# Near keys of a strided attention in tiles of 64 queries by 60 keys instead of 128 by 108

## The reference

```python
def _strided_allowed(S):
    i = jnp.arange(S)[:, None]
    j = jnp.arange(S)[None, :]
    return (j % STRIDE == 0) | (jnp.abs(i - j) <= LOCAL)
scores = jnp.einsum('bhqd,bhkd->bhqk', q, k) / jnp.sqrt(jnp.asarray(D, x.dtype))
scores = jnp.where(allowed, scores, -jnp.inf)
attn = jax.nn.softmax(scores, axis=-1)
out = jnp.einsum('bhqk,bhkd->bhqd', attn, v)
```

## Time and profile before

| | |
|---|---|
| median of 3 runs | 1085.3 us |
| the profiled execution, its own time | 1086.01 us |
| its span, first to last instruction | 1084.2 us |
| TensorE (matmuls) busy | 1028.3 us, 95% |
| VectorE busy | 933.8 us, 86% |
| ScalarE busy | 839.8 us, 77% |
| GpSimd busy | 251.2 us, 23% |
| chain that ended last | PE 76%, DVE 12%, issue 7%, DMA 2%, ACT 2% |

### The profile page before, as it was taken

The page is one execution under the profiler, slowest core; times in us unless marked ns, Lnnn a source line. Parts: engine busy times, 40 slices in busy tenths (PEclk is TensorE's granted clock), DMA queues, the critical chain, the costliest instruction groups (busy, mean ns, idle before and its releaser), DMA issues.

```text
span 1084.2 us, 27687 instructions
## 1 busy us (share of the span) xinstructions
PE 1028.3 (95%) x10694; PEld 462.7 (43%) x10695; DVE 933.8 (86%) x1162; ACT 839.8 (77%) x1590; POOL 251.2 (23%) x387
## 2 busy tenths in 40 slices
PE   4999999699999999999999999999999999999898
PEld 2666666233333333333333333333333333333487
DVE  6989897889999999999999999999999999999133
ACT  4667674288888888888888888888888888888600
POOL 2444453012212121221212122212121222212100
PEclk9999999599999999999999999999999999999999
DMA  6787878213223333333333333323343332231166
GB/s 197 227 254 252 262 250 274 54 46 88 85 83 90 98 85 93 102 91 99 97 96 109 98 99 95 104 84 108 91 113 88 105 91 82 86 85 58 48 236 239
DMA packets 166777, 134.07 MB, mean 124 GB/s; under 512 B 70492, under 2 KB 145884, under 8 KB 166636
## 3 DMA queue, kind: packets, MB, share of 16 engines
q1 hardware_dynamic: 163912, 128.06, 39.3%
q10 hardware_dynamic: 2736, 4.26, 1.2%
HBM read 71.13 MB, written 59.84 MB: 121 GB/s over the span
## 4 chain that ended last, share of the span: by engine, by line
PE 76%; DVE 12%; issue 7%; DMA 2%; ACT 2%; DVEq 0%; ACTq 0%
PE ps_attend L1228 17%; PE ps_attend L1145 12%; DVE peak_far L1087 10%; PE ps_attend L1186 10%; PE ps_project L621 7%; PE ps_attend L1235 6%; PE ps_attend L1308 5%; PE ps_attend L1156 4%; PE ps_project L679 4%; PE ps_attend L1197 3%; PE ps_project L594 3%; PE ps_attend L1163 3%; PE ps_attend L1204 2%; DMA sums<-out_rows 2%; PE ps_project L656 1%
## 5 line engine op out<-in xcount | busy, mean ns | idle before, releaser
L1087 DVE TENSOR_REDUCE peak_far<-ps_attend 128x2 f32<-128x1024 f32 x512 | 608.5, 1220 | 41.0 <-PE ps_attend L1186 30.8
L1028 ACT ACTIVATE probs<-ps_attend 128x512 f32<-128x512 f32 x1024 | 541.1, 597 | 49.5 <-PE ps_attend L1145 46.3
L1228 PE MATMUL ps_attend<-probs,v_op 128*17 128x512 f32 x2048 | 270.1, 600 | 0.5 <-issue 0.5
L1145 PE MATMUL ps_attend<-q_op,k_op 51*128 51x512 f16 x1024 | 252.1, 387 | 4.9 <-ACT probs L1028 3.3
L1186 PE MATMUL ps_attend<-k_op,q_op 48*128 48x512 f16 x1024 | 189.6, 388 | 26.1 <-DVE peak_far L1087 15.5
L1033 ACT ACTIVATE probs<-ps_attend 108x512 f32<-108x512 f32 x256 | 138.7, 594 | 34.6 <-PE ps_attend L1163 34.6
L1145 PEld LDWEIGHTS ps_attend<-q_op,k_op 51*128 51x128 f16 x1024 | 76.8, 93 | 193.9 <-ACT probs L1028 137.4
L894 POOL CAST negmax<-peak 128x16 bf16<-128x16 f32 x64 | 12.6, 196 | 609.6 <-DVE peak L1070 609.6
L1090 DVE TENSOR_REDUCE peak_near<-ps_attend 128x8 f32<-128x864 f32 x128 | 131.0, 1023 | 10.5 <-PE ps_attend L1204 10.4
L885 POOL TENSOR_TENSOR out_rows<-out_rows,share_rows 128x512 f32<-128x512 f32 x64 | 81.4, 1272 | 66.1 <-DMA share_rows<-shares_dram 64.0
L621 PE MATMUL ps_project<-xT_parts,w_parts 128*128 128x512 f16 x384 | 90.6, 387 | 2.1 <-DVE xT_parts L465 2.1
(11 more groups left out here) (91 smaller groups left out, 937.4 us busy)
## 6 DMA issues: line engine op xcount, KB each, us to landing
share_rows<-shares_dram SPq DMA_DIRECT2D x64, 256.0 KB
attn_dram<-out_rows SPq DMA_DIRECT2D x64, 256.0 KB, 5.5
q_dram<-qk_parts SPq DMA_DIRECT2D x48, 256.0 KB, 4.7
k_dram<-qk_parts SPq DMA_DIRECT2D x48, 256.0 KB, 2.7
q_op<-q_dram SPq DMA_DIRECT2D x128, 96.0 KB, 2.4
k_op<-k_dram SPq DMA_DIRECT2D x64, 144.0 KB, 3.1
v_dram<-v_sb SPq DMA_DIRECT2D x16, 544.0 KB, 3.0
base<-in_x SPq DMA_DIRECT2D x16, 512.0 KB, 4.7
```

The source lines that it names most:

```text
L1028: ins = nc.scalar.activation(probs[:, r, h], ps_s[st.bank(kind)], ACT.Exp, scale=undo)
L1087: ins = nc.vector.tensor_reduce(peak_far[:, :, p, tile], banks, AX_X, ALU.max)
L1145: nc.tensor.matmul(bank, k[half(f, KM), keys], q[half(f, KM), p], start=True, stop=True).then_inc(s_ready, 1)
L1228: ins = nc.tensor.matmul(ps_o[h * VW:h * VW + VR], v[:, r, h * VR:(h + 1) * VR], probs[:, r, h], start=(r == 0), stop=False)
```

## The change

Near keys are handled by half tiles: 64 queries have 60 near keys (`NEAR`), so that a block of scores is 64 by 60 and takes a quarter of the array (64 rows by 64 columns). One near unit holds all four tiles of the step, 960 columns for DVE instead of twice 864; one block of near scores holds the exponentials of four heads in two banks of 128 partitions instead of four of 108 (half tiles of one head on each half of the partitions). In `weigh`, v stands for each half tile beside zeros on the other half of the partitions, so that near rounds multiply 128 rows by 64 columns. `SCORE_PAIRS` and `MAXIMA` lose one near entry each; AHEAD goes from 5 to 4 and TURN from 8 to 7.

The keys of both heads of the pair lie in another order, with the far keys between, and the six places at each end are copies of far keys, which POOL makes (`set_edges`): four copies in a row, once for each group of heads, that is in every fourth step. v is loaded in seven transfers instead of four, and POOL zeroes its two buffers once.

```diff
-AHEAD = 5
-TURN = 8
+AHEAD = 4
+TURN = 7
 MAXIMA = (
-    ("far", 2, 1), ("far", 1, 0), ("far", 0, 0), ("near", 0), ("far", 2, 0),
-    ("far", 3, 1), ("far", 1, 1), ("far", 3, 0), ("near", 1), ("far", 0, 1),
+    ("far", 2, 1), ("far", 1, 0), ("far", 0, 0), ("far", 2, 0),
+    ("near",), ("far", 3, 1), ("far", 1, 1), ("far", 3, 0), ("far", 0, 1),
 )
+        def set_edges(st):
+            k, it = k_op[st.parity(2)], st.iteration(2)
+            pool.wait_ge(k_loaded[st.parity(2)], 16 * 2 * 2 * PAIRS * (st.half_iteration(2) + 1))
+            edges = ((0, strided(0)), (SK - WPAD, strided(1)))
+            for i, (f, (to, of)) in enumerate(itertools.product(range(2), edges)):
+                nc.gpsimd.tensor_copy(k[half(f), to:to + WPAD], k[half(f), of:of + WPAD]).then_inc(edges_ready, 1)
+                pool.wait_ge(edges_ready, 4 * it + i + 1)
...
+            if st.n >= 0 and st.exists(2) and st.queries(2) == 0:
+                pool.wait_ge(negmax_ready, st.at(2))
+                set_edges(st)
...
-        def score_near(st, i):
+        def score_near(st):
+            banks = [free_score(st, ("near", f)) for f in range(2)]
+            for sub, f in itertools.product(range(2), range(2)):
+                nc.tensor.matmul(banks[f][half(sub, SUB)], near_one[half(f)], near_q[half(f)], start=True, stop=False)
+            for p, t in itertools.product(range(PAIRS), range(TT)):
+                for sub, f in itertools.product(range(2), range(2)):
+                    at = window(p, st.queries() * TT + t) + sub * SUB_STEP
+                    to = (p * TT + t) * SUB
+                    ins = nc.tensor.matmul(banks[f][half(sub, NEAR), to:to + SUB], k[half(f, KM), at:at + NEAR],
+                                           q[half(f, KM), p, t * P + sub * SUB:t * P + (sub + 1) * SUB], start=False,
+                                           stop=(p == PAIRS - 1 and t == TT - 1))
...
+            if st.queries(2) == 0:
+                pe.wait_ge(edges_ready, 4 * (st.iteration(2) + 1))
             if 2 * n + 2 > U_BANKS:
                 pe.wait_ge(u_used, 2 * n + 2 - U_BANKS)
...
+                for t, sub in itertools.product(tiles, range(2)):
+                    block = NS // P + 2 * (st.queries(d) * TT + t) + sub
                     for h in range(HG):
+                        at, to = (h // 2 * TT + t) * SUB, t * P + sub * SUB
+                        ins = nc.tensor.matmul(ps_o[h * VW:h * VW + VR, to:to + SUB], v[:, block, h * VR:(h + 1) * VR],
+                                               probs[:, r, h % 2, at:at + SUB], start=False,
+                                               stop=(t == TT - 1 and sub == 1))
...
             far(1, 0)
-            near_unit(0)
             far_unit(2, 0)
             far(1, 1)
             weigh_last(4)
-            near(0)
+            near()
+            near_unit()
             far_unit(3, 1)
-            far_unit(1, 1)
             far(2, 0)
             weigh_own(0)
             maxima()
+            far_unit(1, 1)
             far(3, 1)
             far_unit(3, 0)
-            near_unit(1)
             far(3, 0)
             weigh_own(1)
-            near(1)
             far_unit(0, 1)
```

More of the change, by code:

```diff
@@ L287, in gpsimd_project @@
             nc.gpsimd.memset(zeros, 0.0).then_inc(zeros_set, 1)
[L288 to L290 removed]
             nc.gpsimd.memset(keep["negmax"][:], 0.0).then_inc(pads_set, 1)
+            nc.gpsimd.memset(keep["v_op"][:, NS // P:, :], 0.0).then_inc(keep["v_zeroed"], 1)
             nc.gpsimd.memset(v_sb[:, 0, :, :, D:VR], 1.0).then_inc(v_set, 1)
@@ L699 @@
 ROUNDS = NS // P + 1
[L700 removed]
+UNITS = TT * PAIRS + 1
 S_BANKS, U_BANKS = 3, 4
@@ L1210, in near_probs @@
-        def near_probs(h, t):
-            at = (t % 2 * PAIRS + h // 2) * P
-            return probs[0:WIN, ROUNDS - 1, t // 2 * 2 + h % 2, at:at + P]
+            for sub, f in itertools.product(range(2), range(2)):
+                nc.tensor.matmul(banks[f][half(sub, SUB), 0:PAIRS * TT * NEAR], near_q[half(f), 0:SUB],
+                                 near_k[half(f)],
+                                 start=True, stop=False)
+            for p, t in itertools.product(range(PAIRS), range(TT)):
+                for sub, f in itertools.product(range(2), range(2)):
+                    at = window(p, st.queries(2) * TT + t) + sub * SUB_STEP
+                    to = (p * TT + t) * NEAR
+                    ins = nc.tensor.matmul(banks[f][half(sub, SUB), to:to + NEAR],
+                                           q[half(f), p, t * P + sub * SUB:t * P + (sub + 1) * SUB],
+                                           k[half(f), at:at + NEAR], start=False,
+                                           stop=(p == PAIRS - 1 and t == TT - 1))
+                    if p == PAIRS - 1 and t == TT - 1 and sub == 1:
+                        ins.then_inc(u_ready, 1)
@@ L1223, in weigh @@
                 else:
-                    nc.tensor.matmul(ps_o, keep["ident_bf"][:], mask_k[:, 0:CH], start=True, stop=True)
+                    nc.tensor.matmul(ps_o, keep["ident_bf"][:], near_q[:], start=True, stop=True)
             if r < ROUNDS - 1:
@@ L1244, in far_unit, with near_unit @@
                 unit(st, ("far", tile, p))
-            def near_unit(tiles):
-                unit(st, ("near", tiles))
+            def near_unit():
+                unit(st, ("near",))
             def far(r, p):
```

142 lines of the change are left out of this document (64 added, 78 removed).

## The result

The changed kernel takes **1107.45 us** (median of four runs, 1105.81 to 1108.39) against 1085.82 us of the kernel before on the same chip (1085.21 to 1086.64): 1.0197 times as long, 95% interval 1.0179 to 1.0215. That is slower, clear of the noise, as forecast, and 9 us above the forecast of 1098. The profiled execution took 1108.39 us (span 1106.6), 22.4 more than that of before.

A forecast was written before the change was run, and what follows sets the result against it. No single engine was taken as the bound, but a chain of waits across TensorE, ACT and DVE. The terms -3 + 24 - 5 - 3 = +13 us on 1086.0 gave 1099, or 1098 against the runs' median; range 1064 to 1135.

The forecast's parts named there:

- my own case: Whole kernel: the main forecast of 1098 us, own range 1083 to 1122, chance 0.60.
- The new step: Ordinary step: the chain across three engines takes 12.54 us, a gain of 0.05 a step, 3 us over some 60.
- DVE's saved work: DVE in each step: 0.87 us less work, which becomes a wait for the near unit's matmuls.
- The small matmuls: Near weighing, near scores and near unit on TensorE: 1.02, 0.51 and 0.48 us, the low end of the prices.
- By columns: Small matmuls on TensorE: time goes with the number of columns, not the number of matmuls.
- The edges: Every fourth step: the near unit waits for POOL's four copies, 1.6 us 15 times, +24 us (18 to 25).
- The sums: DVE's waits for the sums' transfer, 7.1 us in all, shrink: 5 us off (0 to 7).
- Start and end: Before the first joined maxima one near unit less (-1 us); in the last three steps one near block less (-2).
- Priced by count: Rival on small matmuls: they cost as much as larger ones, 2.1 us more a step, some 1224 us; chance 0.13.
- The chain is shorter: Rival on the step: without one wait for an exponential it takes 11.96 us, the kernel 1063; chance 0.19.
- F11's wait: Far scores late in the step: their second half waits for an exponential, and TensorE stands 0.6 us.
- The edges don't hold NU: Rival on fourth steps: copies are ready in time for the near unit, 1079 us; chance 0.08.

The follow-up runs named there:

- cover: edges_early with one pair of far scores moved from ahead of a far unit to behind the turned maxima; 1068.3 us, 0.9841 times the kernel before.
- edges_early: The changed kernel with POOL's four edge copies ahead of the split of the maxima instead of behind it; 1084.35 us, 0.9983 times the kernel before.
- n_twice: The changed kernel with the near block of scores, masks included, issued twice, the second over the first; 1147.94 us in a single run.
- copies_twice: The changed kernel with each of the four edge copies made twice, behind the split of the maxima; 1129.65 us in a single run.
- kept_busy: The changed kernel with twelve far matmuls run while TensorE stands for the late copies, then overwritten; 1100.78 us, 1.0145 times the kernel before.
- order_b: edges_early with the whole step in another order, maxima joined after one unit; 1059.02 us, 0.9745 times the kernel before.
- order_b_first: order_b with SyncE issuing the turned maxima's transfer ahead of the second piece of k or v loads; 1042.24 us, 0.9589 times the kernel before.
- order_c: edges_early with another whole-step order, near unit and joined maxima early, SyncE untouched; 1030.89 us, 0.9502 times the kernel before.

## Why the prediction was right, and where it fell short

The time lies inside the range of my own case (1083 to 1122), and most links of its working were measured as they were forecast; one term was missing.

- **The new step: right.** 12.54 forecast, 12.49 measured, -6 us over 60 steps instead of -3. It holds link by link, counted from NU's reduce at 701.28: U30's reduce at 3.60 (3.61 forecast), F11's second half at 9.78 (9.88), W4 at 10.10 (10.20). The wait that it was built on is there: F11's second half comes 0.63 behind the first (0.61 forecast). cover, where that wait is gone, has steps that are 0.28 shorter, though how much of this is the wait's is not shown. DVE's saved work became the wait for NU, 1.60 us (1.3 forecast). edges_early is 0.2% from the kernel before (0.9967 to 1.0): in this order that saving bought next to nothing.
- **The small matmuls: right for their time.** By columns: W4 1.01 (1.02 forecast), N 0.54 (0.51), NU 0.57 up to the unit behind it (0.48). The 32 blocks of N start within 0.30 us (700.15 to 700.45). By the overhead in the Trainium skill, TensorEngine Tiling (Array Packing), section Instruction Overhead, taken one block after another, they would need 0.80 by estimate; the trace doesn't agree with that for blocks on four tiles of the array. What I left out is the supply of instructions, which n_twice shows at 1.0 us a stand, 13 times. In the changed kernel ordinary steps that are longer than the others cost some 3 us more than in the kernel before; the profile names the supply for 1.0 us of this, and for the rest it is not shown.
- **The edges: right in place and size.** 1.66 us, 15 times, +25 (1.6 and +24 forecast). The four copies take 0.92 (1.05 taken, 0.7 to 1.1 as bounds), edges_early takes the cost away and copies_twice adds 1.0 a step.
- **The sums: right.** Their waits in the steps are gone (-5 forecast), and 4.7 us of them come back once the copies are early.
- **Start and end:** -3 (up to the third joined maxima) and 0 (from the last joined maxima on, where both kernels take 79.4 us) in place of -1 and -2.
- **The term that failed: the price of the stand itself.** "1.6 us, 15 times, +24 us" counted only the time that NU comes later. The stand also lowers TensorE's clock behind it: 8.4 us in this execution, shown by kept_busy (no fall where TensorE has work in the gap) and by copies_twice (twelve falls instead of five). My sum had no such term, since the kernel before never stands that long in its steps (1.22 us at most). With it and the longer ordinary steps, -6 + 25 - 5 + 8 + 3 - 3 = +22 against the 22.4 measured.
- **The rivals.** "Priced by count" falls with N and NU at half a microsecond. "The chain is shorter" falls with F11's wait and the step of 12.49; cover and the other orders show what a shorter chain is worth. "The edges don't hold NU" falls with the 15 waits.

## What to carry to other kernels

Less work on engines that wait was worth next to nothing here until the chain between them was shortened too: the same change stands 22 us over the kernel before in one order and, with early copies, 55 us under it in another. A small operation that is made late and that the next link of the chain needs (four copies of 0.23 us) cost its place in that chain each time, 1.66 us; put it where its input is ready, not where its output is used. Where a wait makes TensorE stand, count the clock behind it as well: here a fall cost 1 to 2 us.

## What the hardware showed that I had not expected

**The clock after a stand.** In the traces of these kernels, in the steps from 240 us on, TensorE fell to 0.50 of its clock only behind stands of 1.53 us and more: behind 5 of the 15 stands of the changed kernel (1.47 to 1.53 us), behind 12 of 15 of some 2.5 us in copies_twice, behind one of 1.91 in edges_early and two in order_b (1.66 and 2.03). The clock stayed at 1.00 during the stand and fell up to 1.7 us after work had begun again, in copies_twice in two places almost at once; then it was half for about 3 to 7 us of nearly full work. Not each such stand was followed by a fall (1.83 in order_b, 1.92 in order_b_first and 1.60 in order_c were not); n_twice and cover, whose longest stands are 1.42 and 1.43, have none. What decides in the single case stayed open.

**The supply of instructions.** In blocks of small matmuls TensorE can stand for its next instructions: 18 us in n_twice with 39301 instructions in all, 1.0 us by name in the changed kernel with 34694 (some 4 us if all that its ordinary steps are longer than 12.49 is put down to it, which is not shown). The number alone does not set it: with the same 34679 instructions it is 1.6 us in edges_early and 5.8 in order_c. Where in the program such a stand comes was not studied.
